# A fused recurrent block on eight cores: the quantisation steps of a period in another order, the absolute value queued one step later

## The chip, the cores and the metric

The kernel runs on the 8 cores of one Trainium2 chip. Each core works on its own 4096 of the 32768 rows; the weights go to all. The metric is the device time in microseconds of the slowest core.

## The reference

Cut to what is computed:

```python
xn = layernorm(x)
# attention half: s
q, k, v = split(rmsnorm(xn) @ qkv_w.T)
q, k = exp(-0.5 * q * q), exp(-0.5 * k * k)
attn = q @ (k.T @ v) / (q @ k.sum() + 1e-6)          # 16 heads, over 2048 rows
s1 = xn + gamma * (attn @ proj_w.T + proj_b)
s  = s1 + gamma * (gelu(rmsnorm(s1) @ conv1_w.T + conv1_b) @ conv2_w.T + conv2_b)
# feed-forward half: g, every operand rounded to a 4-bit grid in blocks of 16
scale = max(max(abs(xb)) / 6, 1e-12)
q4(x) = GRID[searchsorted(MID, abs(xb / scale))] * sign(xb) * scale
h = silu(q4(xn) @ q4(w_gate).T) * (q4(xn) @ q4(w_up).T)
g = silu(q4(h) @ q4(w_down).T)
out = x + s * g
```

## The kernel before

A core holds 32 tiles of 128 rows. The work has three stages.

Stage one, up to about 400 us of the profiled span, makes keys, values and queries (`kv_group`, `q_group`, L628 and L659) with TensorE. ScalarE empties each bank: a square (L643, L676) and an exponential (L645, L679), or a copy (L652). For each x tile VectorE makes statistics (L454 to L457), GpSimd the reciprocal root (L461 to L473), ScalarE the normalised tile (L480), and the SyncE queue transposes it (L484) and loads the next x tile.

Stage two, up to about 1026 us, goes over eight groups of four tiles: `conv1` (L962), `conv2` (L979) and, for the group ahead, attention (L863), its normalisation on VectorE (L882 to L889), the projection (L914) and its sum on VectorE (L921). The projection of a group waits for the last L889 of that group's tiles, since both use the same banks.

Stage three is the feed-forward half: gate and up (L1168), the product of both on VectorE (L1186), its quantisation, and down (L1213).

The 4-bit rounding runs as a stream of tasks beside this. A task is one tile of 128 x 1024 or 128 x 768, of a weight or of x, and takes seven VectorE steps in two halves. `stage1`, with its tile called y (buffer xf): the block maximum (L238), the scale (L242), its reciprocal (L245), the division (L247). Then ScalarE makes the absolute value (`coarse`, L256) into gam. `stage2`: a sum that rounds (L266), the remainder (L269), the product with the scale (L272) into ob. `period` (L278) mixes the first half of one task (a) with the second half of the task before (b) by a string of letters, one per step; `mid`, `late_in` and the sending of the finished tile are called at fixed places in it. A buffer xf is free for the next load once L269 is done.

In stages one and two the main program calls `pump(ns)` (L401) between its own groups. It hands out steps until their costs, which each step yields in ns, use up the credit. So every queue's order is fixed when the program is written, and an instruction waits in its engine's queue behind those that were queued before it. There are 85 tasks in these two stages. In stage three `run` takes whole periods; `late[0]` is true there, and `mid` queues the absolute value. A task made from h has a step ahead of L238 (the product of gate and up), so its first half has five steps; 15 tiles of x are quantised only in this stage, with four.

Of the kernel before, what the change touches and what calls it, by code (L numbers as in the profile page):

```python
# [33 lines left out]
class Sched:  # L34
# [29 lines left out]
    def opt(self, name):  # L64

        return name if name in self.ev else None


def build():
# [15 lines left out]
    with ExitStack() as es:  # L85
# [123 lines left out]
        late = [False]  # L209
# [5 lines left out]
        def xbuf(k):  # L215
            return xf4 if xslot(k) == 3 else xf[xslot(k)]

        def xfree(k):

            had = [j for j in range(max(k - 4, 0), k) if xslot(j) == xslot(k)]  # L220
            return opt("q_nq%d" % had[-1]) if had else None


        def bc(ap, nb):
            return ap.rearrange("p n -> p n ()").broadcast_to([P, nb, 16])

        def blk(ap):
            return ap.rearrange("p (n b) -> p n b", b=16)

        def stage1(k, W, first, src_ev):  # L230

            nb = W // 16
            y = xbuf(k)[:, 0:W]
            am, sc_, rc = (z[k % 2][:, 0:nb] for z in (q_am, q_sc, q_rc))
            if first is not None:
                first()
                yield 1250
            S.add("v", lambda v: v.tensor_reduce(am, blk(y), AX, op.max,  # L238
                                                 apply_absolute_value=True),
                  waits=[src_ev, xfree(k)], ev="q_am%d" % k)  # L240
            yield W * 1.06 + 160
            S.add("v", lambda v: v.tensor_scalar(sc_, am, 1.0 / 6.0, 1e-12, op.mult, op.max),  # L242
                  waits=["q_am%d" % k, opt("q_out%d" % (k - 2))], ev="q_sc%d" % k)
            yield 200
            S.add("v", lambda v: v.reciprocal(rc, sc_), waits=["q_sc%d" % k], ev="q_rc%d" % k)  # L245
            yield 700
            S.add("v", lambda v: v.scalar_tensor_tensor(blk(y), blk(y), TIE, bc(rc, nb),  # L247
                                                        op.mult, op.mult),
                  waits=["q_rc%d" % k], ev="q_y%d" % k)
            if not late[0]:  # L250
                coarse(k, W)
            yield W * 1.06 + 160

        def coarse(k, W):

            S.add("sc", lambda s: s.activation(gam[k % 2][:, 0:W], xbuf(k)[:, 0:W], AF.Abs,  # L256
                                               scale=BIG),
                  waits=["q_y%d" % k, opt("q_out%d" % (k - 2))], ev="q_g%d" % k)

        def stage2(k, W, dst, dst_free, post):  # L260

            nb = W // 16
            y = xbuf(k)[:, 0:W]
            sc_ = q_sc[k % 2][:, 0:nb]
            gm_ = gam[k % 2][:, 0:W]
            S.add("v", lambda v: v.scalar_tensor_tensor(y, gm_, FLOOR, y, op.max, op.add),  # L266
                  waits=["q_g%d" % k, "q_y%d" % k], ev="q_t%d" % k)
            yield W * 1.06 + 160
            S.add("v", lambda v: v.scalar_tensor_tensor(gm_, gm_, FLOOR, y, op.max, op.subtract),  # L269
                  waits=["q_t%d" % k], ev="q_nq%d" % k)  # L270
            yield W * 1.06 + 160
            S.add("v", lambda v: v.scalar_tensor_tensor(blk(dst), blk(gm_), -1.0, bc(sc_, nb),  # L272
                                                        op.mult, op.mult),
                  waits=["q_nq%d" % k] + list(dst_free), ev="q_out%d" % k)
            post(k)
            yield W * 1.06 + 160

        def period(a, b, mid, late_in):  # L278

            a = list_steps(a)  # L280
            b = list_steps(b)
            for n, who in enumerate("aabababa" if a.n == 5 else "aababab"):
                src = a if who == "a" else b
                if n == 1:
                    send()
                    mid()
                if n == 5:
                    late_in()
                c = src.step()
                if c:  # L290
                    yield c
            for src in (a, b):
                while True:
                    c = src.step()
                    if c is None:
                        break
                    yield c
# [22 lines left out]
        def xn_task(tk):  # L320

            if tk["tile"] is not None:
                k = tk["k"]
                buf = xf[k % 3][:, 0:tk["W"]]
                t = tk["tile"]
                S.add("sc", lambda s: s.activation(buf, buf, AF.Identity,
                                                   scale=rstd_all[:, t:t + 1],
                                                   bias=mrs_all[:, t:t + 1]),
                      waits=["q_ld%d" % k, "mrs%d" % t], ev="q_xn%d" % k)
                tk["ev"] = "q_xn%d" % k  # L330
# [3 lines left out]
        def send():  # L334

            while unsent:
                unsent.pop(0)()

        def stored(tk):
            def store(k):  # L340
                S.add("sy", lambda s: s.dma_start(out=tk["dst"], in_=ob[k % 2][:, 0:tk["W"]]),
                      waits=["q_out%d" % k], inc="OB%d" % (k % 2), ev="q_st%d" % k)
                S.ev[tk["done"]] = S.ev["q_st%d" % k]

            def post(k):
                unsent.append(lambda: store(k))
            return post

        def both(cur, prev, ahead=None):

            a = b = None
            if cur is not None:
                k = cur["k"]
                a = (5 if "first" in cur else 4,
                     stage1(k, cur["W"], cur.get("first"), cur["ev"]))
            if prev is not None:
                k = prev["k"]  # L360
                if "post" in prev:
                    dst, post = prev["dst"], prev["post"]
                    free = [opt(e) for e in prev["free"]]
                else:
                    dst, free = ob[k % 2][:, 0:prev["W"]], [opt("q_st%d" % (k - 2))]
                    post = stored(prev)
                b = (3, stage2(k, prev["W"], dst, free, post))
            def late_in():
                if ahead is not None:
                    xn_task(ahead)  # L370

            def mid():
                if prev is not None and "q_g%d" % prev["k"] not in S.ev:
                    coarse(prev["k"], prev["W"])

            for c in period(a, b, mid, late_in):
                yield c

        def stream():
# [884 lines left out]
        def run(cur):  # L1264

            for _ in both(cur, prev[0]):
                pass
            prev[0] = cur
# [105 lines left out]
```

How the kernel before makes its waits and increments, by code:

```python
                def body(eng):  # L1324
                    for fn, waits, inc, amt in S.ops[key]:
                        for smn, val in waits:
                            eng.wait_ge(sems[smn], val)
                        ins = fn(eng)
                        if inc is not None and ins is not None:
                            ins.then_inc(sems[inc], amt)
                    if key == "sy":
                        for smn, val in sorted(S.cnt.items()):
                            eng.wait_ge(sems[smn], val)
```

## Time and profile before

| what | us |
|---|---|
| median of 3 runs | 1955.89 |
| the three runs | 1953.26, 1955.89, 2096.47 |
| the profiled execution | 1954.67 |
| its span on the slowest core (core 4) | 1953.1 |
| spans of the 8 cores | 1941.7 to 1953.1 |

The span runs from the first to the last instruction; the profiled execution's time is 1.6 us longer. Engines: PE is TensorE, PEld its weight loads, DVE VectorE, ACT ScalarE, POOL GpSimd, SPq the SyncE queue. In a row of the timeline "[5.52 <-DVE xf L247]" says that the engine sat idle for 5.52 us before this instruction and that L247 on VectorE ended it.

### The profile page before, as it was taken

The numbers are of one execution on the slowest core, as the hardware profiler recorded it, in microseconds if no ns is written. First come the engines' busy times: TensorE is split into PE (matmuls) and PEld (weight loads), VectorE is DVE, ScalarE is ACT, GpSimd is POOL, SyncE is SP. The second block draws the span as 40 slices with busy tenths as digits, with TensorE's granted clock in tenths as the row PEclk, the third lists the DMA queues.
The fourth block names the chain that finished last, engine by engine and source line by source line (L and its number), as shares of the span: only waits on it lengthen the run. The fifth ranks groups of instructions, "written<-read, shape, count | busy, mean of one in ns | idle before, by whom it ended". The sixth has DMA issues, their size and how long they took to land.

```text
span 1953.1 us, 27578 instructions; the slowest of 8 cores (1941.7 to 1953.1 us)
## 1 busy us (share of the span) xinstructions
PE 1852.0 (95%) x8982; PEld 876.4 (45%) x9142; DVE 1631.1 (84%) x1907; ACT 784.9 (40%) x991; POOL 396.5 (20%) x356
## 2 busy tenths in 40 slices
PE   6899999688999999999999999999999999999997
PEld 3344444344444444444444444444444444444443
DVE  5789999868878878778707999999999999999986
ACT  4577686555353353464312222222232222323221
POOL 3246457444252252252200000000000000000000
PEclk9999999899999999999999999999999999999999
DMA  9899898766546547557699333433343333333322
GB/s 304 217 250 251 226 252 244 209 185 170 149 112 194 144 105 184 151 127 197 155 179 189 99 80 104 104 109 76 105 106 90 91 106 89 92 105 101 85 78 68
DMA packets 367261, 287.06 MB, mean 147 GB/s; under 512 B 299024, under 2 KB 308240, under 8 KB 366096
## 3 DMA queue, kind: packets, MB, share of 16 engines
q1 hardware_dynamic: 367120, 285.29, 56.3%
q8 instruction: 75, 1.23, 0.3%
q14 instruction: 66, 0.54, 0.1%
HBM read 153.63 MB, written 59.24 MB: 109 GB/s over the span
## 4 chain that ended last, share of the span: by engine, by line
PE 76%; DVE 6%; issue 6%; DMA 6%; POOL 2%; ACT 2%; SPq 1%; DVEq 0%; ACTq 0%; POOLq 0%
PE PS L1168 31%; PE PS L1213 15%; PE PS L979 11%; PE PS L962 9%; PE PS L914 5%; DMA xa<-x 2%; PE PS L703 1%; PE PS L637 1%; PE PS L671 1%; DVE q_am L238 1%; DVE ob L272 1%; DVE xf L247 1%; DMA wst<-c1T 1%; DMA wqg_h<-ob 1%; PE PS L863 1%
## 5 line engine op out<-in xcount | busy, mean ns | idle before, releaser
L256 ACT ACTIVATE gam<-xf 128x1024 bf16<-128x1024 f32 (+1 forms) x196 | 198.2, 1011 | 502.1 <-DVE xf L247 493.5
L1168 PE MATMUL PS<-wg,xqT 128*128 128x512 bf16 (+1 forms) x1504 | 318.2, 361 | 3.4 <-DVE so L989 1.7
L1168 PE MATMUL PS<-wu,xqT 128*128 128x512 bf16 (+1 forms) x1510 | 317.5, 361 | 1.4
L266 DVE SCALAR_TENSOR_TENSOR xf<-gam,xf 128x1024 f32<-128x1024 bf16 (+1 forms) x196 | 240.5, 1227 | 38.2 <-ACT gam L256 37.9
L272 DVE SCALAR_TENSOR_TENSOR ob<-gam,q_sc 128x1024 bf16<-128x1024 bf16 (+1 forms) x196 | 240.1, 1225 | 4.4 <-DVE gam L269 2.8
L238 DVE TENSOR_REDUCE q_am<-xf 128x64 f32<-128x1024 f32 (+1 forms) x196 | 227.6, 1161 | 18.6 <-DMA xf<-w_gate 4.0
L247 DVE SCALAR_TENSOR_TENSOR xf<-xf,q_rc 128x1024 f32<-128x1024 f32 (+1 forms) x196 | 238.7, 1218 | 1.9
L269 DVE SCALAR_TENSOR_TENSOR gam<-gam,xf 128x1024 bf16<-128x1024 bf16 (+1 forms) x196 | 234.1, 1194 | 2.1
L962 PE MATMUL PS<-xn2T,c1T_s 128*128 128x512 bf16 x1024 | 231.9, 381 | 0.0
L1213 PE MATMUL PS<-wdA,hqT 128*128 128x512 bf16 x998 | 225.4, 380 | 1.8 <-DMA hqT<-ob 0.5
L979 PE MATMUL PS<-c2T_s,hdd 128*128 128x512 bf16 x1000 | 220.9, 379 | 1.3
L1168 PEld LDWEIGHTS PS<-wg,xqT 128*128 128x128 bf16 x1536 | 150.3, 98 | 159.1 <-issue 2.1
L1168 PEld LDWEIGHTS PS<-wu,xqT 128*128 128x128 bf16 x1536 | 150.3, 98 | 153.9
L1178 ACT ACTIVATE sg<-PS 128x1024 f32<-128x1024 f32 (+1 forms) x96 | 90.9, 948 | 182.3 <-PE PS L1168 182.3
L979 PEld LDWEIGHTS PS<-c2T_s,hdd 128*128 128x128 bf16 x1024 | 100.1, 98 | 120.9
L1213 PEld LDWEIGHTS PS<-wdA,hqT 128*128 128x128 bf16 x1024 | 100.5, 98 | 119.4 <-issue 3.1
L962 PEld LDWEIGHTS PS<-xn2T,c1T_s 128*128 128x128 bf16 x1024 | 99.4, 98 | 115.4 <-issue 2.2
L671 PE MATMUL PS<-xn1T,qT_s 128*128 128x512 bf16 x512 | 123.8, 394 | 20.4 <-ACT sq L676 12.6
L842 POOL TENSOR_TENSOR xx<-xx,gb 128x1024 f32<-128x1024 f32 x32 | 83.1, 2606 | 220.4 <-ACT xx L838 220.4
L914 PE MATMUL PS<-projT_s,atzT 128*128 128x512 bf16 x496 | 114.2, 383 | 11.1 <-DVE atz L889 7.3
L1186 DVE TENSOR_TENSOR xf<-PS,sg 128x1024 f32<-128x1024 f32 (+1 forms) x96 | 108.5, 1130 | 14.8 <-PE PS L1168 13.5
L637 PE MATMUL PS<-kT_s,xn1T 128*128 128x512 bf16 x424 | 105.6, 401 | 12.0 <-ACT xn L480 4.2
(91 smaller groups left out, 1840.8 us busy)
## 6 DMA issues: line engine op xcount, KB each, us to landing
xx<-x SPq DMA_DIRECT2D x32, 512.0 KB, 5.1
xf<-x SPq DMA_DIRECT2D x32, 512.0 KB, 4.4
xr<-x SPq DMA_DIRECT2D x32, 512.0 KB, 4.4
out<-xr SPq DMA_DIRECT2D x31, 512.0 KB, 3.2
xa<-x SPq DMA_DIRECT2D x30, 512.0 KB, 6.2
stg<-qkvT SPq DMA_DIRECT2D x24, 512.0 KB, 13.0
xf<-w_gate SPq DMA_DIRECT2D x22, 512.0 KB, 7.9
xf<-w_up SPq DMA_DIRECT2D x22, 512.0 KB, 6.4
```

Of the source, the lines that this page charges most:

```text
L238: S.add("v", lambda v: v.tensor_reduce(am, blk(y), AX, op.max, apply_absolute_value=True), waits=[src_ev, xfree(k)], ev="q_am%d" % k)
L247: S.add("v", lambda v: v.scalar_tensor_tensor(blk(y), blk(y), TIE, bc(rc, nb), op.mult, op.mult), waits=["q_rc%d" % k], ev="q_y%d" % k)
L256: S.add("sc", lambda s: s.activation(gam[k % 2][:, 0:W], xbuf(k)[:, 0:W], AF.Abs, scale=BIG), waits=["q_y%d" % k, opt("q_out%d" % (k - 2)) ...
L266: S.add("v", lambda v: v.scalar_tensor_tensor(y, gm_, FLOOR, y, op.max, op.add), waits=["q_g%d" % k, "q_y%d" % k], ev="q_t%d" % k)
L269: S.add("v", lambda v: v.scalar_tensor_tensor(gm_, gm_, FLOOR, y, op.max, op.subtract), waits=["q_t%d" % k], ev="q_nq%d" % k)
L272: S.add("v", lambda v: v.scalar_tensor_tensor(blk(dst), blk(gm_), -1.0, bc(sc_, nb), op.mult, op.mult), waits=["q_nq%d" % k] + list(dst_fr ...
L671: S.add("pe", lambda pe, ic=ic: pe.matmul(bk, qT[:, ic, P * qc:P * (qc + 1)], xn1T[:, h:h + 4, ic, :], start=(ic == 0), stop=(ic == 7)), w ...
L914: S.add("pe", lambda pe, ic=ic, hh=hh, bk=bk: pe.matmul(bank(bk), atzT[:, t % 4, ic, :], projT[:, ic, 512 * hh:512 * (hh + 1)], start=(ic ...
L962: S.add("pe", lambda pe, ic=ic: pe.matmul(bk, c1T[:, ic, P * oc:P * (oc + 1)], xn2T[:, :, ic, :], start=(ic == 0), stop=(ic == 7)), waits= ...
L979: S.add("pe", lambda pe, ic=ic: pe.matmul(bank(bks[hh]), hdd[:, ic, P * (t % 4):P * (t % 4 + 1)], c2T[:, ic, 512 * hh:512 * (hh + 1)], sta ...
L1168: S.add("pe", lambda pe, wts=wts, bi=bi, j=j, b0=b0, ic=ic: pe.matmul(bank(b0 + j, GB[bi][1]), xqT[t % 3][:, ic, :], wts[bi][:, ic, :], st ...
L1213: S.add("pe", lambda pe, kc=kc, hh=hh, wt=wt, b0=b0: pe.matmul(bank(b0 + hh), hqT[t % 2][:, kc, :], wt, start=(kc == 0), stop=(kc == 21)), ...
```

## The change

Two edits. The string of a period whose first half has four steps goes from `aababab` to `aaababb`: the reciprocal comes ahead of the older task's rounding sum, the division ahead of its remainder, and the remainder stands right ahead of its product. Periods with five steps keep their order. In the first two stages the absolute value of a task is no longer queued with its division but one step later, after the older task's remainder and ahead of its product.

```diff
@@ stage1
                   waits=["q_rc%d" % k], ev="q_y%d" % k)
-            if not late[0]:
-                coarse(k, W)
             yield W * 1.06 + 160
@@ period
-        def period(a, b, mid, late_in):
+        def period(a, b, mid, late_in, absolute):
...
-            for n, who in enumerate("aabababa" if a.n == 5 else "aababab"):
+            for n, who in enumerate("aabababa" if a.n == 5 else "aaababb"):
                 src = a if who == "a" else b
                 if n == 1:
                     send()
                     mid()
                 if n == 5:
                     late_in()
+                if n == 6:
+                    absolute()
                 c = src.step()
@@ both
-            for c in period(a, b, mid, late_in):
+            def absolute():
+                if cur is not None and not late[0]:
+                    coarse(cur["k"], cur["W"])
+
+            for c in period(a, b, mid, late_in, absolute):
                 yield c
```

The lines of the changed kernel differ: L254 is its absolute value, L264, L267 and L270 its rounding sum, remainder and product; L238, L242, L245 and L247 keep their numbers.

VectorE in stage one, one period and the start of the next, before (xf and gam are the task's buffers, bst and mv_all the statistics of an x tile):

```order
L238 TENSOR_REDUCE q_am1_46<-xf1_84 128x64
L242 TENSOR_SCALAR q_sc1_48<-q_am1_46 128x64
L266 SCALAR_TENSOR_TENSOR xf0_83<-gam0_87,xf0_83 128x1024
L245 RECIPROCAL q_rc1_50<-q_sc1_48 128x64
L454 BN_STATS bst0_60<-xa0_92 128x6
L456 BN_STATS bst0_60<-xa0_92 128x6
L457 BN_AGGR mv_all_51<-bst0_60 128x2
L269 SCALAR_TENSOR_TENSOR gam0_87<-gam0_87,xf0_83 128x1024
L247 SCALAR_TENSOR_TENSOR xf1_84<-xf1_84,q_rc1_50 128x1024
L272 SCALAR_TENSOR_TENSOR ob0_89<-gam0_87,q_sc0_47 128x1024
```

And the same place in the changed kernel:

```order
L238 TENSOR_REDUCE q_am1_46<-xf1_84 128x64
L242 TENSOR_SCALAR q_sc1_48<-q_am1_46 128x64
L245 RECIPROCAL q_rc1_50<-q_sc1_48 128x64
L264 SCALAR_TENSOR_TENSOR xf0_83<-gam0_87,xf0_83 128x1024
L461 BN_STATS bst0_60<-xa0_92 128x6
L463 BN_STATS bst0_60<-xa0_92 128x6
L464 BN_AGGR mv_all_51<-bst0_60 128x2
L247 SCALAR_TENSOR_TENSOR xf1_84<-xf1_84,q_rc1_50 128x1024
L267 SCALAR_TENSOR_TENSOR gam0_87<-gam0_87,xf0_83 128x1024
L270 SCALAR_TENSOR_TENSOR ob0_89<-gam0_87,q_sc0_47 128x1024
```

The reciprocal now follows the scale it reads and the product follows the remainder it reads; the statistics stay in their place.

ScalarE's queue around the absolute value that starts at 241.30 us in the profile of before (sq, pq and xn1 belong to the key and query groups):

```order
L676 ACTIVATE sq_101<-PS 128x512
L679 ACTIVATE pq0_102<-sq_101 128x512
L652 CAST vext1_100<-PS 128x8x64
L256 ACTIVATE gam0_87<-xf0_83 128x1024
L480 ACTIVATE xn1_1_95<-xa1_93,m1_r_57,vr_r_55 128x1024
L652 CAST vext1_100<-PS 128x8x64
L676 ACTIVATE sq_101<-PS 128x512
```

The same place in the changed kernel, where L683, L686, L659 and L487 are these operations:

```order
L683 ACTIVATE sq_101<-PS 128x512
L686 ACTIVATE pq0_102<-sq_101 128x512
L659 CAST vext1_100<-PS 128x8x64
L487 ACTIVATE xn1_1_95<-xa1_93,m1_r_57,vr_r_55 128x1024
L659 CAST vext1_100<-PS 128x8x64
L254 ACTIVATE gam0_87<-xf0_83 128x1024
L683 ACTIVATE sq_101<-PS 128x512
```

The absolute value has moved behind the normalised tile and a copy. Of the 85 absolute values of the first two stages 52 stand behind one to three more instructions of the main program than before, and 33 stand where they stood. The order on TensorE, GpSimd and the SyncE queue is the same in both kernels.

## Rows read from the trace of the kernel before

**Rows 1.** The page, busy time and share of each engine.

```profile
PE 1852.0 (95%) x8982; PEld 876.4 (45%) x9142; DVE 1631.1 (84%) x1907; ACT 784.9 (40%) x991; POOL 396.5 (20%) x356
```

**Rows 2.** Windows: length, busy of PE, PEld, DVE, ACT, POOL, PE clock, DMA, GB/s.

```profile
60.00:400.00 340.00, 301.91 (x1458) 138.69 (x1481) 303.20 (x344) 240.44 (x354) 169.28 (x180) 0.95 0.88 236
400.00:1026.00 626.00, 600.76 (x2921) 279.80 (x2961) 453.76 (x578) 268.15 (x344) 210.53 (x130) 0.99 0.62 157
1026.00:1953.00 927.00, 909.75 (x4390) 438.57 (x4480) 844.78 (x940) 249.46 (x256) 0.00 (x0) 1.00 0.39 99
```

**Rows 3.** Waits 60 to 400 us: who waited for whom, total us, times, longest.

```profile
PE PS L671 <- ACT sq L676: 12.6, 3, 8.6
...
ACT gam L256 <- DVE xf L247: 35.4, 18, 5.5
...
DVE bst L454 <- DMA xa<-x: 10.4, 3, 5.5
DVE xf L266 <- ACT gam L256: 9.4, 5, 5.3
```

**Rows 4.** Timeline of DVE (start us, us, engine, line, operation): one period of stage one.

```profile
175.53 0.20 DVE L242 TENSOR_SCALAR q_sc<-q_am 128x64 f32<-128x64 f32 x1
175.64 1.22 DVE L266 SCALAR_TENSOR_TENSOR xf<-gam,xf 128x1024 f32<-128x1024 bf16 x1
176.78 0.55 DVE L245 RECIPROCAL q_rc<-q_sc 128x64 f32<-128x64 f32 x1
177.24 1.16 DVE L269 SCALAR_TENSOR_TENSOR gam<-gam,xf 128x1024 bf16<-128x1024 bf16 x1
178.32 1.21 DVE L247 SCALAR_TENSOR_TENSOR xf<-xf,q_rc 128x1024 f32<-128x1024 f32 x1
```

**Rows 5.** Timeline of DVE in stage three, dependent neighbours.

```profile
1734.07 0.96 DVE L269 SCALAR_TENSOR_TENSOR gam<-gam,xf 128x768 bf16<-128x768 bf16 x1
1735.20 0.96 DVE L272 SCALAR_TENSOR_TENSOR ob<-gam,q_sc 128x768 bf16<-128x768 bf16 x1 [0.17 <-DVE gam L269]
...
1741.26 0.20 DVE L242 TENSOR_SCALAR q_sc<-q_am 128x64 f32<-128x64 f32 x1
1741.56 0.55 DVE L245 RECIPROCAL q_rc<-q_sc 128x64 f32<-128x64 f32 x1
```

**Rows 6.** Timeline of ACT and PE in stage one, absolute values and waits.

```profile
241.30 1.06 ACT L256 ACTIVATE gam<-xf 128x1024 bf16<-128x1024 f32 x1 [5.52 <-DVE xf L247]
242.26 1.23 ACT L480 ACTIVATE xn<-xa,m_r,vr_r 128x1024 bf16<-128x1024 f32 x1
...
267.35 1.89 PE L671 MATMUL PS<-xn1T,qT_s 128*128 128x512 bf16 x8 [2.73 <-ACT sq L676]
...
306.84 5.23 PE L671 MATMUL PS<-xn1T,qT_s 128*128 128x512 bf16 x16 [2.57 <-ACT sq L643]
...
367.16 1.06 ACT L256 ACTIVATE gam<-xf 128x1024 bf16<-128x1024 f32 x1 [4.23 <-DVE xf L247]
...
368.85 3.61 PE L671 MATMUL PS<-xn1T,qT_s 128*128 128x512 bf16 x16 [1.23 <-ACT sq L676]
```

**Rows 7.** Timeline of stage two: DVE and PE at two attention tails.

```profile
546.22 3.37 DVE L247 SCALAR_TENSOR_TENSOR xf<-xf,q_rc 128x1024 f32<-128x1024 f32 x1
...
551.79 3.40 PE L914 MATMUL PS<-projT_s,atzT 128*128 128x512 bf16 x15 [2.17 <-DVE atz L889]
...
844.36 1.23 DVE L889 TENSOR_TENSOR atz<-PS,zz 128x1024 bf16<-128x1024 f32 x1 [0.17 <-DVE zz L886]
...
846.80 3.40 PE L914 MATMUL PS<-projT_s,atzT 128*128 128x512 bf16 x15
```

**Rows 8.** Waits of DVE, 500 to 1000 us.

```profile
DVE xx L921 <- PE PS L914: 76.0, 24, 4.0
...
DVE den L882 <- PE PS L863: 3.2, 7, 0.8
...
DVE xf L266 <- ACT gam L256: 1.5, 2, 1.3
```

## The prediction

> **What bounds the kernel now.** I read the page first: TensorE is busy 95% of the span, VectorE 84%, ScalarE 40% [rows 1]. A share over three unlike stages says little, so the next view is the table of windows, cut where the work changes [rows 2]. Stage one (60 to 400 us) has TensorE busy 301.9 of 340 us, at a granted clock of 0.95, and VectorE 303.2, so neither runs through. Stage two (400 to 1026 us) has TensorE busy 600.8 of 626. Stage three (1026 us to the end) has it busy 909.8 of 927, with VectorE at 844.8. What the change can give or take is thus some 38 us of TensorE idle in stage one, 25 in stage two and 17 in stage three, plus what the lower clock costs.
>
> The waits say who holds whom in stage one [rows 3]. ScalarE sat before the absolute value (L256) 18 times, 35.4 us in all, until the division (L247) on VectorE was done. TensorE waited 12.6 us in three pieces for ScalarE's squares (L676), which empty its banks. The timeline joins the two: at 367.16 the absolute value starts after 4.23 us of waiting, and at 368.85 TensorE starts after waiting 1.23 us for the square behind it. At 241.30 the wait was 5.52 us, and behind it in the same queue stands the normalisation that starts at 242.26 [rows 6]. Its transpose feeds TensorE, and the SyncE queue holds weight loads behind that transpose; TensorE waited 2.73 us at 267.35 [rows 6].
>
> **The change on VectorE: the new neighbours.** All seven VectorE steps of a period stay; their order changes. In the old order only the scale (L242) stood right behind the instruction it needs. In the new one the reciprocal (L245) stands right behind the scale it needs, and the last product (L272) right behind the remainder it needs (L269). What that costs the trace shows. Scale to the independent step behind it takes 0.11 us from start to start (175.53 to 175.64), and independent long ones start 0.08 us before the end of the one ahead (177.24 + 1.16 = 178.40, next start 178.32) [rows 4]. In stage three the dependent pairs already exist: scale to reciprocal takes 1741.56 - 1741.26 = 0.30 us, and remainder to product leaves 1735.20 - 1734.07 - 0.96 = 0.17 us idle [rows 5]. So a new scale-reciprocal pair costs 0.30 - 0.11 = 0.19 us, and a new remainder-product pair 0.17 + 0.08 = 0.25 us.
>
> The order of instructions tells how many pairs arise, since other work falls between some of them. Stage one: 37 and 28, so 37 x 0.19 + 28 x 0.25 = 14.0 us. Stage two: 45 and 30, so 16.1 us. Stage three, where only the 15 tiles quantised late use this order: 15 and 15, so 6.6 us. Together 36.7 us more of VectorE time; the bounds of what reaches the end are 0 and all of it.
>
> The row decides this price, for the pairs are in the trace. The Trainium skill (VectorE: DVE Perf Modes, section "The DRAIN you can't avoid") says that a semaphore between two VectorE instructions costs nothing extra, measured on chained copies. By that rule the new neighbours would add 0 instead of 36.7 us. The 0.17 us idle before L272 against an overlap of 0.08 us speaks against it here.
>
> **How much of it counts.** Stage one: VectorE idles there too, and idle time that another engine sets can swallow the gaps. It waited 10.4 us for x tiles and 9.4 us for absolute values [rows 3]. The x loads follow tiles that depend on VectorE's own statistics, so I let half of that swallow gaps, 5.2 us. Of the 9.4 us, one wait of 5.3 us comes from ScalarE standing behind TensorE and its absolute value does not move; the other 4.1 us shrink, because the path on VectorE from division to the rounding (L266) now has the remainder and the reciprocal more in it (1.16 + 0.55 us [rows 4]); I take 3.2. The other edge of this, that the absolute value is queued later, could bring new waits of up to the same size; with the longer path beside it I take nothing.
>
> Then the relief on ScalarE. Of the 85 absolute values of the first two stages 52 move, behind one to three other instructions, and every division stands one VectorE step (1.16 us) earlier in relation to its period. At 241.30 and 367.16 the absolute value moves behind the normalisation and behind a square and an exponential: these start up to 6.5 and 4.2 us earlier, so the TensorE waits of 2.73 and 1.23 us [rows 6] can go. I take these, 4.0 us; bounds 0 and the whole 12.6 us. Stage one: 14.0 - 5.2 - 3.2 - 4.0 = +1.6 us.
>
> Stage two: no wait of TensorE there is for ScalarE; the rows are for VectorE. In each group of four tiles VectorE ends by waiting for the projection (76.0 us in 24 waits [rows 8]), which swallows all gaps before it. What counts is the run from there to the last normalisation of attention (L889), for which TensorE waits before L914: 2.17 us at 551.79 [rows 7]. That run holds 5 and 3 new pairs in the median group, 1.7 us. Against it stand the waits of VectorE inside the run, 3.2 us in 7 for attention and 1.5 for absolute values [rows 8], over six runs. At 844.36 the step ends at 845.59 and TensorE starts its next work only at 846.80 without a wait [rows 7], so a run without a stall has about 1 us to spare. Two runs with a stall and no cover pay 1.3 and 1.1, the others 0.2 or less, one of them because a rounding step moves behind its last L889: +2.5 us. SyncE's order is unchanged, but its x and weight loads wait for L269, now one step (1.2 us) later; three or four buffers cover that, and I count 0.
>
> Stage three: 6.6 us more on VectorE against 82 us of its idle time: 0. Also the steps with a first product keep their order.
>
> Sum: 1.6 + 2.5 = +4.1 us on the profiled execution's 1954.67 us gives 1958.8; that execution lies 1.2 us under the median of 1955.89, which is within the spread. I forecast 1959 us. There is scatter as well: a division took 3.37 us at 546.22 where another takes 1.21 [rows 4, 7], some 2 us right in a tail; the new order changes which step such a delay hits, with either sign. The likeliest case's own range is 1950 to 1970.
>
> **Rivals.** (A) ScalarE's relief wins. VectorE's gaps vanish in its idle time and the three waits of 12.6 us go: 1954.7 - 12.6 = 1942 us. For it: the 35.4 us of waiting are real, and both large ones let something through that TensorE needs. Against: a wait for VectorE in a stage where VectorE is nearly full comes back at the next thing that waits for it, here the statistics.
> (B) The new neighbours cost nothing. Then only what is relieved is left, 3.2 us of VectorE's waits and 4.0 us of TensorE's: 1954.7 - 3.2 - 4.0 = 1947.5 us. For it: in stage one the pairs are new, and rows 5 are from stage three. Against: the same instructions with the same operands make the pairs there. This is what the Trainium skill's rule (VectorE: DVE Perf Modes, "The DRAIN you can't avoid") would come to.
> (C) Slower: VectorE paces every stage. If it had no idle time that swallows, all 36.7 us would reach the end: 1991.4 us. Each new stall can add a stretch at half clock: 16 matmuls took 5.23 us at 306.84 against 3.61 at 368.85 [rows 6], 1.6 us; six tails with one make 9.7, so 2001 us. It decides once VectorE's idle time in a stage is less than its gaps; stage one has 37 us of idle against 14.0, so only a chain through the statistics could bring it there.
> (D) The change does nothing: the order of instructions shows that it does move them, so this can only come as a cancelling of terms, inside the forecast.
>
> **How the numbers follow.** Forecast 0.52; A 0.25; B 0.13; C 0.10, mostly in partial form (half of the 36.7 us, 1973). About what a measurement of this kernel can tell from no change is 2%, 39 us: faster means under 1917, slower over 1995. Faster by that needs more than all of stage one's TensorE idle: 0.01. Slower needs all of C: 0.02. Within: 0.97. The range takes A in from below and the partial C from above: 1940 to 1976.
>
> **What would show it.** In the changed profile: reciprocals 0.30 us behind scales and 0.17 us of idle before L270 (the old L272) about 58 times before 1026 us; VectorE busy time as before, with its idle time smaller elsewhere; ScalarE's wait at L254 (the old L256) before 400 us down from 35.4 to some 20 us; the TensorE wait for L914's counterpart near 551 us some 1 us longer. I am wrong if stage one ends over 5 us earlier (A or B; B if the idle before L270 is absent), or if it ends over 10 us later (C).

## The result and the profile after

| | before | after |
|---|---|---|
| median, us | 1955.89 | 1973.95 (4 runs, 1973.37 to 1974.52) |
| ratio | 1 | 1.0094, 95% interval 1.0077 to 1.0111 |
| the profiled execution, us | 1954.67 | 1973.93 |
| its span on the slowest core, us | 1953.1 (core 4) | 1972.4 (core 0) |
| spans of the 8 cores, us | 1941.7 to 1953.1 | 1964.1 to 1972.4 |

Some executions of a kernel are disturbed and longer; a ratio leaves them out and a median does not, so where the two disagree below, the ratio is to be read.

The change made the kernel about 18 us slower. It was predicted to cost 4 us, so the direction was right and the size was wrong. The time lies inside the whole range of 1940 to 1976 us, whose upper end stood for rival C, and above the 1950 to 1970 us of the likeliest case. By the page, VectorE's busy time rose by 35.4 us against [rows 1], with the same 1907 instructions:

```profile
PE 1851.2 (94%) x8982; PEld 876.1 (44%) x9142; DVE 1666.5 (84%) x1907; ACT 783.8 (40%) x991; POOL 388.4 (20%) x356
```

The windows of the changed kernel answer to [rows 2] (the third ends later, as the kernel does):

```profile
60.00:400.00 340.00, 295.95 (x1426) 136.72 (x1448) 307.70 (x343) 234.63 (x343) 168.81 (x180) 0.94 0.85 230
400.00:1026.00 626.00, 588.48 (x2877) 273.28 (x2917) 479.09 (x576) 274.85 (x355) 204.28 (x130) 0.99 0.62 154
1026.00:1970.00 944.00, 927.63 (x4472) 446.59 (x4562) 850.43 (x945) 247.41 (x256) 0.00 (x0) 1.00 0.40 100
```

In the first window VectorE is 4.5 us busier and has done one instruction less; TensorE has done 32 matmuls fewer. In the second VectorE is 25.3 us busier for two instructions less. So the extra busy time is not more work. Between the two landmarks that follow, the same 574 steps last 487.3 us before and 507.0 us after when their durations are added up, 19.7 us more; the rest is lost overlap, since a step that waits for its neighbour no longer starts before that one's end.

Two landmarks split the loss: the first L889 (here L896) after stage one, and the first product of gate and up (L1186, here L1193), which opens stage three. From the timeline of VectorE, before:

```profile
405.89 1.35 DVE L889 TENSOR_TENSOR atz<-PS,zz 128x384 bf16<-128x384 f32 x3 [4.10 <-DMA phi_h<-pqx]
...
1033.59 1.23 DVE L1186 TENSOR_TENSOR xf<-PS,sg 128x1024 f32<-128x1024 f32 x1 [7.32 <-PE PS L1168]
```

and after:

```profile
415.56 1.35 DVE L896 TENSOR_TENSOR atz<-PS,zz 128x384 bf16<-128x384 f32 x3 [5.80 <-DMA phi_h<-pqx]
...
1052.84 1.23 DVE L1193 TENSOR_TENSOR xf<-PS,sg 128x1024 f32<-128x1024 f32 x1 [7.32 <-PE PS L1175]
```

On these two cores, the slowest of each profiled execution, stage one ends 9.7 us later and stage two takes 9.6 us more. Cores differ by some us, so from here on a landmark is the median over the eight cores. The first stands at 400.5 us before and 413.0 after (+12.5). Stage two, the median of each core's distance between the landmarks, takes 627.8 us before and 637.5 after (+9.6). Each kernel has one profile. The kernels below whose stage one is that of the kernel before end it at 400.0 to 401.4 us, and those with the whole change in it at 409.8 to 413.0, so its cost there is 9 to 12 us. The two pairs that share their stage two, uncut, differ by 0.7 us or less. The last product of gate and up starts 19.6 us later after (1942.0 against 1922.4 us on the two profiled cores), where the first started 19.3 us later: stage three neither adds nor gives back.

The new neighbours look as predicted. One period of stage one after, VectorE's timeline:

```profile
177.28 1.22 DVE L267 SCALAR_TENSOR_TENSOR gam<-gam,xf 128x1024 bf16<-128x1024 bf16 x1
178.67 1.23 DVE L270 SCALAR_TENSOR_TENSOR ob<-gam,q_sc 128x1024 bf16<-128x1024 bf16 x1 [0.17 <-DVE gam L267]
...
182.45 0.14 DVE L242 TENSOR_SCALAR q_sc<-q_am 128x64 f32<-128x64 f32 x1
182.70 0.55 DVE L245 RECIPROCAL q_rc<-q_sc 128x64 f32<-128x64 f32 x1
183.17 1.16 DVE L264 SCALAR_TENSOR_TENSOR xf<-gam,xf 128x1024 f32<-128x1024 bf16 x1
```

The idle 0.17 us stands before L270 55 times ahead of 1026 us. After a scale of 0.20 us the reciprocal starts 0.28 to 0.30 us behind it, 67 times.

The waits of stage one after (60 to 400 us, who waited for whom, total us, times, longest) answer to [rows 3]:

```profile
ACT xn L487 <- POOL mrs_all L480: 30.3, 13, 7.5
...
ACT gam L254 <- DVE xf L247: 20.2, 17, 3.4
...
PE PS L678 <- DMA xn1T<-xn: 11.9, 1, 11.9
DVE xf L264 <- ACT gam L254: 9.7, 5, 6.9
PE PS L644 <- DMA xn1T<-xn: 9.3, 3, 5.6
...
PE PS L678 <- ACT sq L683: 4.5, 1, 4.5
...
DVE bst L461 <- DMA xa<-x: 2.4, 2, 1.8
```

The relief of ScalarE came: its wait before the absolute value fell from 35.4 us [rows 3] to 20.2. But it now waits 30.3 us for the statistics of an x tile before it can normalise, and TensorE waits 21.2 us (11.9 and 9.3) for the transposed tile behind that. The rows for the same two places before are these:

```profile
ACT xn L480 <- POOL mrs_all L473: 11.1, 5, 4.2
```

```profile
PE PS L637 <- DMA xn1T<-xn: 0.7, 2, 0.5
```

Stage two shows something else. VectorE's timeline around 850 us:

```profile
844.64 3.38 DVE L267 SCALAR_TENSOR_TENSOR gam<-gam,xf 128x1024 bf16<-128x1024 bf16 x1
...
849.77 2.51 DVE L270 SCALAR_TENSOR_TENSOR ob<-gam,q_sc 128x1024 bf16<-128x1024 bf16 x1
852.21 1.21 DVE L238 TENSOR_REDUCE q_am<-xf 128x64 f32<-128x1024 f32 x1
...
855.92 3.22 DVE L264 SCALAR_TENSOR_TENSOR xf<-gam,xf 128x1024 f32<-128x1024 bf16 x1
...
860.90 2.55 DVE L247 SCALAR_TENSOR_TENSOR xf<-xf,q_rc 128x1024 f32<-128x1024 f32 x1
```

and GpSimd's of the same time:

```profile
844.48 2.46 POOL L849 TENSOR_TENSOR xx<-xx,gb 128x1024 f32<-128x1024 f32 x1 [27.57 <-ACT xx L845]
848.86 2.35 POOL L849 TENSOR_TENSOR xx<-xx,gb 128x1024 f32<-128x1024 f32 x1 [1.92 <-ACT xx L845]
855.72 2.35 POOL L849 TENSOR_TENSOR xx<-xx,gb 128x1024 f32<-128x1024 f32 x1 [4.51 <-ACT xx L845]
860.02 2.35 POOL L849 TENSOR_TENSOR xx<-xx,gb 128x1024 f32<-128x1024 f32 x1 [1.96 <-ACT xx L845]
```

Each of the four long steps (all but L238) starts while GpSimd adds, and ends a full step after the addition, within 0.16 us: 844.48 + 2.46 = 846.94, plus 1.16 gives 848.10, against an end at 848.02. That fits a step that stands still until GpSimd is done. I call such a step stretched when it took over 0.25 us more than usual. From 400 to 1030 us there are 23 with 32.7 us of excess before, and 34 with 52.1 us after: 19.4 us more. The profiled core of before has the least of its eight cores; the medians over the cores are 36.0 and 52.3 us, 16.3 us more. Stage one has stretched steps too, 31 us before and 33 us after, beside another long step of GpSimd, a product (L568, here L575), so little of its loss comes from them. In TensorE's waits of stage two (400 to 1026 us) this stands before the attention groups, before:

```profile
PE PS L863 <- DVE atz L889: 8.5, 5, 4.6
```

and after:

```profile
PE PS L870 <- DVE atz L896: 21.4, 12, 6.3
```

### The profile page after: what moved, and what is told of

It reads as the page before. It is cut to its first block, busy times and chain, and to the rows that moved or that the text cites. A ratio compares the mean times of both kernels' runs of the same rounds, so it can differ in the third digit from the quotient of the medians.

```text
span 1972.4 us, 27583 instructions; the slowest of 8 cores (1964.1 to 1972.4 us)
## 1 busy us (share of the span) xinstructions
PE 1851.2 (94%) x8982; PEld 876.1 (44%) x9142; DVE 1666.5 (84%) x1907; ACT 783.8 (40%) x991; POOL 388.4 (20%) x356
## 4 chain that ended last, share of the span: by engine, by line
PE 68%; DVE 13%; issue 10%; DMA 4%; ACT 2%; POOL 2%; SPq 1%; DVEq 0%; ACTq 0%; POOLq 0%
PE PS L1175 31%; PE PS L1220 15%; PE PS L986 7%; PE PS L969 6%; PE PS L921 5%; DVE gam L267 2%; DVE q_am L238 2%; PE PS L710 1%; DVE xf L247 1%; DMA phi_h<-pq 1%; DVE xf L264 1%; DVE atz L896 1%; PE PS L678 1%; DVE so L996 1%; DVE ob L270 1%
## 5 line engine op out<-in xcount | busy, mean ns | idle before, releaser
L254 ACT ACTIVATE gam<-xf 128x1024 bf16<-128x1024 f32 (+1 forms) x196 | 197.8, 1009 | 512.9 <-DVE xf L247 512.9
L264 DVE SCALAR_TENSOR_TENSOR xf<-gam,xf 128x1024 f32<-128x1024 bf16 (+1 forms) x196 | 239.6, 1222 | 31.2 <-ACT gam L254 31.2
L270 DVE SCALAR_TENSOR_TENSOR ob<-gam,q_sc 128x1024 bf16<-128x1024 bf16 (+1 forms) x196 | 240.1, 1225 | 17.3 <-DVE gam L267 14.9
L247 DVE SCALAR_TENSOR_TENSOR xf<-xf,q_rc 128x1024 f32<-128x1024 f32 (+1 forms) x196 | 251.3, 1282 | 1.9
L267 DVE SCALAR_TENSOR_TENSOR gam<-gam,xf 128x1024 bf16<-128x1024 bf16 (+1 forms) x196 | 249.9, 1275 | 2.4 <-DVE q_sc L242 0.4
L238 DVE TENSOR_REDUCE q_am<-xf 128x64 f32<-128x1024 f32 (+1 forms) x196 | 227.6, 1161 | 18.2 <-ACT xf L329 4.1
L678 PE MATMUL PS<-xn1T,qT_s 128*128 128x512 bf16 x512 | 122.7, 392 | 16.8 <-DMA xn1T<-xn 11.9
L973 ACT ACTIVATE hdd<-PS,c1b_fm 128x512 bf16<-128x512 f32 x128 | 86.9, 680 | 99.3 <-PE PS L969 99.1
L921 PE MATMUL PS<-projT_s,atzT 128*128 128x512 bf16 x496 | 112.6, 379 | 12.8 <-DVE atz L896 7.6
```

The lines of the kernel that those rows point to most:

```text
L678: S.add("pe", lambda pe, ic=ic: pe.matmul(bk, qT[:, ic, P * qc:P * (qc + 1)], xn1T[:, h:h + 4, ic, :], start=(ic == 0), stop=(ic == 7)), w ...
L921: S.add("pe", lambda pe, ic=ic, hh=hh, bk=bk: pe.matmul(bank(bk), atzT[:, t % 4, ic, :], projT[:, ic, 512 * hh:512 * (hh + 1)], start=(ic ...
```

## The experiments

All twelve ran beside the kernel before on their chip, whose median was 1952.7 us (new order alone, the first run of the later absolute value, and both whole kernels with GpSimd cut), 1954.9 (other neighbours, no neighbours, small steps, change in stage one only) and 1956.6 (the others). "Stage one" is the first landmark and "stage two" the distance between the two, medians over the cores of one profiled execution. "Stretched" is the excess in stage two on the profiled core, and behind it the median over the eight cores.

| kernel | us | ratio, 95% interval | stage one | stage two | stretched |
|---|---|---|---|---|---|
| before | 1955.9 | 1 | 400.5 | 627.8 | 32.7, 36.0 |
| after | 1974.0 | 1.0094, 1.0077 to 1.0111 | 413.0 | 637.5 | 52.1, 52.3 |
| new order alone | 1970.2 | 1.0084, 1.0066 to 1.0102 | 407.0 | 635.9 | 50.2, 47.2 |
| later absolute value alone | 1950.5 | 0.9971, 0.9956 to 0.9987 | 399.8 | 621.9 | 32.5, 31.9 |
| before, GpSimd cut | 1933.8 | 0.9907, 0.9891 to 0.9924 | 400.0 | 606.8 | 0, 0 |
| after, GpSimd cut | 1943.3 | 0.9958, 0.9943 to 0.9974 | 409.8 | 609.1 | 0, 0 |
| other neighbours, late division | 1976.6 | 1.0121, 1.0091 to 1.0151 | 409.9 | 639.4 | 46.6, 42.4 |
| no neighbours | 1982.9 | 1.0037, 1.0014 to 1.0059 | 405.3 | 623.5 | 29.9, 30.9 |
| small steps added | 1990.1 | 1.0188, 1.0159 to 1.0217 | 415.3 | 648.9 | 59.9, 57.7 |
| change in stage one only | 1965.7 | 1.0061, 1.0034 to 1.0087 | 410.0 | 627.1 | 35.8, 33.6 |
| change from stage two on | 1969.3 | 1.0067, 1.0045 to 1.0090 | 401.4 | 638.1 | 47.5, 47.2 |
| the same, GpSimd cut | 1938.1 | 0.9904, 0.9871 to 0.9938 | 400.1 | 610.2 | 0, 0 |
| absolute value two steps later | 1968.8 | 1.0064, 1.0041 to 1.0087 | 405.1 | 636.6 | 46.8, 47.4 |

**The two edits apart.** The new string with the absolute value where the old kernel queues it (ScalarE's order up to the end of stage two is then that of before in all but 8 of some 700 places):

```diff
+            for n, who in enumerate("aabababa" if a.n == 5 else "aaababb"):
                 if n == 5:
                     late_in()
+                    absolute()
-                if n == 6:
-                    absolute()
```

> The new order of VectorE's steps, with the absolute value at the place in ScalarE's queue where it stood before. Theory V (the new order on VectorE costs the time: two dependent pairs per period, and more collisions with GpSimd in stage two): this alone gives the whole loss, 1970 to 1980 us, and the TensorE waits for the attention's normalisation (L896) come to 20 us or more. Rival Q (the absolute value, queued later, holds up what is behind it): this alone is near the kernel before, 1950 to 1962 us.

It took 1970.17 us: the order alone carries nearly all of the loss. TensorE's waits for L896's counterpart were 20.0 us, as expected. In stage one its waits are these, with the square, at 4.7 us, as low as in the changed kernel though the absolute value has not moved:

```profile
PE PS L677 <- DMA xn1T<-xn: 10.4, 1, 10.4
...
PE PS L677 <- ACT sq L682: 4.7, 2, 4.4
...
PE PS L643 <- DMA xn1T<-xn: 4.1, 2, 2.7
```

The other half, the old string with the absolute value one step behind the division:

```diff
-            for n, who in enumerate("aabababa" if a.n == 5 else "aaababb"):
+            for n, who in enumerate("aabababa" if a.n == 5 else "aababab"):
```

> VectorE's steps in the order of before, the absolute value in ScalarE's queue where the change puts it. Theory V: no loss, a small gain from ScalarE's relief, 1945 to 1956 us, with ScalarE's wait before the absolute value under 30 us up to 400 us. Rival Q: 1962 to 1975 us.

Its two shortest runs took 1946.44 and 1947.24 us beside a before of 1952.69, too few for a ratio. The same kernel, run once more:

> The same kernel as in the first look at the absolute value alone: the old string, the absolute value queued one step behind the division. There its one run of use took 1946.44 us and its trace ended stage one 4 us and stage two 7.5 us ahead of before. If that was more than scatter: a ratio of 0.995 to 0.998, its interval below 1. If scatter: an interval that holds 1.

That gave a ratio of 0.9971 (0.9956 to 0.9987), 1950.49 us: this half of the change is a small gain, and the version is faster than both kernels. In stage one no gain can be told from scatter (399.8 against 400.5 us); it is in stage two, 621.9 against 627.8. ScalarE's waits there (400 to 1026 us) read

```profile
ACT gam L254 <- DVE xf L247: 70.3, 15, 7.7
```

where before had

```profile
ACT gam L256 <- DVE xf L247: 99.2, 22, 7.7
```

That these shorter waits are the gain is not shown: the changed kernel has 64.9 us there and is slower, and TensorE's waits for L889 and its counterpart are the same in both kernels, 15.8 us before and 15.6 here.

In the changed order the same edit brings no gain: new order alone against the whole change stands at 407.0 and 635.9 against 413.0 and 637.5 us. The ratios overlap, so only the stage-one figures say that it costs there, by some 3 to 6 us: the two other profiles with the whole change in stage one stand at 410.0 and 409.8 us.

**One step further.** The call goes behind the loop, so the absolute value is queued after the older task's product:

```diff
                 if c:
                     yield c
+            absolute()
```

> The old string, the absolute value queued two steps behind the division, after the product and ahead of the next task's block maximum. If what helps is that ScalarE's other work gets past a waiting absolute value: as good as one step, 1944 to 1950 us, or a little better. If the later absolute value makes the next rounding sum on VectorE wait (between them stand only the block maximum and the scale, 1.3 us): VectorE's waits for gam grow from 9.4 us to over 20 us before 400 us, and the time is 1955 to 1970 us.

It was slower, ratio 1.0064. VectorE's and ScalarE's waits before 400 us show that both ends lose:

```profile
ACT xn L486 <- POOL mrs_all L479: 32.8, 14, 6.0
...
DVE xf L264 <- ACT gam L254: 24.7, 10, 6.2
```

One step is a gain and two are a loss. In stage one the next rounding sum (L264) is then too close behind: VectorE's wait for the absolute value is 24.7 us where it was 9.4. Stage two is 8.8 us longer, with 20.9 us of that wait against 1.5 and with more stretched steps.

**GpSimd's additions cut.** In the kernel before and in the changed kernel the bias additions of the attention and of the convolution half are cut to 8 of 1024 columns; the other columns' sums lack the bias.

```diff
-            S.add("gp", lambda p: p.tensor_tensor(xb[:], xb[:], gb[:], op.add),
+            S.add("gp", lambda p: p.tensor_tensor(xb[:, 0:8], xb[:, 0:8], gb[:, 0:8], op.add),
...
-            S.add("gp", lambda p: p.tensor_tensor(x2b[:], x2b[:], gc2[:], op.add),
+            S.add("gp", lambda p: p.tensor_tensor(x2b[:, 0:8], x2b[:, 0:8], gc2[:, 0:8], op.add),
```

> The kernel before, with GpSimd's two large additions of stage two (gb and gc2 to the x tiles) cut to 8 of 1024 columns; the rest of those sums is left out. Theory V-collision: VectorE's long steps in stage two (32.7 us over their usual time before) all but go, and 3 to 8 us of the time with them: 1945 to 1952 us. It is the base for the next kernel.

> The changed kernel with the same additions cut to 8 columns. If collisions with GpSimd carry about half of the loss, it stands 8 to 12 us over the kernel before with the same cut. If the dependent pairs alone carry it, the distance stays at 18 us or more. If collisions in stage two carry all of it, the distance is what stage one lost, 5 to 6 us.

The cut was expected to gain the kernel before 3 to 8 us and gained 18. It removes more than the stretching, since GpSimd has some 140 us less to do in stage two, so not all of the 18 us need be stretched steps. The gap between old and new shrank from 18 to 9.5 us, and it sits mostly in stage one (409.8 against 400.0 us). Stage two differs by 2.4 us, 609.1 against 606.8, where it differed by 9.6, though the new neighbours are all there.

**Other neighbours, and none.** The string aaabbab has as many dependent neighbours, but others (the remainder behind its rounding sum), and leaves the division late.

```diff
-            for n, who in enumerate("aabababa" if a.n == 5 else "aababab"):
+            for n, who in enumerate("aabababa" if a.n == 5 else "aaabbab"):
```

> The kernel before with the string aaabbab: the division stays one step ahead of the product as before and the absolute value is queued with it, but the reciprocal stands right behind its scale and the remainder right behind its rounding sum. So it has about as many dependent neighbours as the changed kernel and none of its earlier division. Theory V (the dependent neighbours cost VectorE time, and that time reaches the end): about 0.19 + 0.25 us in each of some 80 periods again, 1960 to 1972 us beside a before of about 1953. Theory W (the loss of the changed order comes from where the division and the remainder stand against GpSimd and the buffers, not from neighbours): 1950 to 1956 us.

The string abababa has none.

```diff
-            for n, who in enumerate("aabababa" if a.n == 5 else "aababab"):
+            for n, who in enumerate("aabababa" if a.n == 5 else "abababa"):
```

> The kernel before with the string abababa: no step of a period stands behind the step that it reads. Against before it loses the dependent neighbour pair of block maximum and scale, against the changed kernel two more pairs. The division becomes the last step, the product stands ahead of it. Theory V: 0.1 to 0.2 us a period less on VectorE than before, so 1945 to 1953 us, unless the absolute value that is now queued last makes the rounding sum wait. Theory W: no forecast from the pairs; the time depends on the steps' places, 1953 to 1975 us, since the division is later still.

With other neighbours the loss is the changed kernel's or a little more (1.0121; somewhat over the range expected), so it does not hang on the earlier division. Without neighbours the ratio is 1.0037, a small loss where the theory allowed a small gain: stage two is 4.3 us shorter, stage one 4.8 us longer, and VectorE waits 21.1 us for absolute values before 400 us where it waited 9.4 [rows 3], the exception that the expectation named. The two stages leave 0.5 us; the ratio stands for 7 us, with an interval from 3 to 12, and its profiled execution was the shortest of its runs. So 2 us or more are without a place.

**Small steps added.** The old order, with two small VectorE steps behind each reciprocal of stages one and two:

```diff
+            if not late[0]:
+                S.add("v", lambda v: v.tensor_scalar(am, sc_, 1.0, None, op.mult),
+                      waits=["q_sc%d" % k], ev="q_pad%d" % k)
+                S.add("v", lambda v: v.tensor_scalar(am, am, 1.0, None, op.mult),
+                      waits=["q_pad%d" % k], ev="q_pae%d" % k)
```

> The kernel before, with two small VectorE steps of 128 x 64 behind each reciprocal in the first two stages (they copy the scale into the block maximum's buffer, which nothing reads any more): about 0.3 to 0.5 us more on VectorE in each of 85 tasks, 26 to 42 us in all, with the order of all other steps as before. Theory V: as much VectorE time as the changed kernel's 30 us of gaps in these stages, so 1962 to 1975 us. If VectorE's idle time swallows such time, as my forecast had it: 1953 to 1958 us.

One undisturbed period in its timeline:

```profile
178.61 0.55 DVE L245 RECIPROCAL q_rc<-q_sc 128x64 f32<-128x64 f32 x1
179.08 0.13 DVE L247 TENSOR_SCALAR q_am<-q_sc 128x64 f32<-128x64 f32 x1
179.31 0.19 DVE L249 TENSOR_SCALAR q_am<-q_am 128x64 f32<-128x64 f32 x1
179.43 1.22 DVE L274 SCALAR_TENSOR_TENSOR gam<-gam,xf 128x1024 bf16<-128x1024 bf16 x1
```

From the reciprocal to the next long step it takes 179.43 - 178.61 = 0.82 us; in the kernel before it is 0.46 (176.78 to 177.24 [rows 4]). So 0.36 us times 85 tasks is 31 us, as much as the 30.1 us of new gaps in these stages, with nothing reordered. The time went up by 1.88%, some 37 us, more than the 9 to 22 us expected. VectorE's idle time before 1026 us does not swallow such time: stage one is 14.9 us longer, with 13.7 us of added steps and some 5 us more of stretched ones; stage two is 21.1 us longer, with 17 us added and 22 to 27 us more of stretched ones (59.9 us on the profiled core, 57.7 in the median). How the 21.1 us divide between the two this run can't tell. Thirteen of the 36 stretched steps of stage two are the small steps themselves, and stage one has such a case too, which took 2.11 us instead of 0.13:

```profile
170.32 2.11 DVE L247 TENSOR_SCALAR q_am<-q_sc 128x64 f32<-128x64 f32 x1
```

**One stage at a time.** The change in full for the first 38 tasks only, and for the others only. The absolute value stays with the division where the old string holds.

```diff
-            for n, who in enumerate("aabababa" if a.n == 5 else "aaababb"):
+            for n, who in enumerate("aabababa" if a.n == 5 else "aaababb" if new else "aababab"):
...
-                if n == 6:
+                if n == 6 and new:
                     absolute()
...
-            for c in period(a, b, mid, late_in, absolute):
+            for c in period(a, b, mid, late_in, absolute,
+                            cur is not None and cur["k"] < 38):
```

> The change in full for the first 38 tasks (stage one), and the old string and the old place of the absolute value for all later ones. By the traces of before and after the changed kernel is 6 to 10 us behind at the first attention group and 17 to 20 us behind at the end of stage two. Theory of a chain in each stage: 1959 to 1963 us beside a before of about 1953, so that the rest, 8 to 12 us, belongs to stage two. My forecast's split had +1.6 us for stage one: 1954 to 1956. If a late stage one is swallowed by stage two: 1951 to 1955.

> The old string and the old place of the absolute value for the first 38 tasks, the change in full for all later ones: the complement of the run with the change in stage one alone, which was 0.61% over before (0.34 to 0.87%), some 12 us. If the two stages' losses add up, this one is the rest of the changed kernel's 0.94%: 0.3 to 0.6%, so 6 to 11 us over a before of about 1954. My forecast's step for this stage was +2.5 us. If the loss of stage two arises only where stage one has run late: within 3 us of before.

> The change from the 39th task on only, and GpSimd's bias additions cut to 8 of 1024 columns (the bias is left out of the other columns' sums), to be set beside the kernel before with the same cut, 1933.75 us. Theory X (in stage two the new order costs through VectorE steps that are stretched while GpSimd adds; the gaps alone are swallowed there): 1932 to 1937 us. Theory Y (the 16 us of gaps reach the end by themselves): 1940 to 1946 us.

The stages are separate. The first run lost 9.5 us in stage one and nothing in stage two; the second lost 0.9 us in stage one, which is scatter, and 10.3 us in stage two. Their ratios, 0.61% and 0.67%, are both somewhat over what was expected and add up to more than the 0.94% of the whole change, which their intervals allow. The third, with GpSimd cut, stands beside the kernel before with the same cut: 610.2 against 606.8 us in stage two, and ratios of 0.9904 and 0.9907, too coarse to show 3 us. Its 1938.1 us lies between the ranges of both theories. No core of the kernel before with the cut took over 608.7 us in stage two, and no core of this one under 609.2. So the gaps of stage two alone cost some 2 to 3 us (2.4 and 3.4 in the two pairs), a small part of their 16 us; with GpSimd's additions the same change costs 9.6 to 10.3 us. TensorE's waits for L889's counterpart before the attention groups tell the same: 4.9 us with the cut before, 6.1 and 6.2 with the cut and the change, against 8.5 and 21.4 without the cut. The windows of the two cut kernels (400 to 1026 us), the kernel before first,

```profile
400.00:1026.00 626.00, 616.51 (x3053) 287.30 (x3053) 432.64 (x587) 272.30 (x346) 70.87 (x130) 1.00 0.66 163
```

and the change from stage two on,

```profile
400.00:1026.00 626.00, 613.93 (x3036) 285.70 (x3036) 435.47 (x584) 271.16 (x346) 69.28 (x130) 0.99 0.64 161
```

have VectorE's busy time within 3 us of each other, where the uncut kernels lie 25.3 us apart. Added up between the landmarks, their steps last 454.3 and 454.7 us.

## Why the prediction was wrong, point by point

**The price of a neighbour: right.** 0.19 and 0.25 us came out of the trace, and the new gaps look as forecast (0.17 us of idle 55 times against 58 forecast). Rival B falls with it, and so does, in this kernel, the rule that it rested on (the Trainium skill, VectorE: DVE Perf Modes, "The DRAIN you can't avoid"): the step that waits for its neighbour's semaphore starts 0.17 us after it, where an independent one starts 0.08 us before its end. In the line view of stage one L245 had 0.1 us of idle before it and now has 3.9, and L270 has 4.1 us from L267:

```profile
L270 DVE SCALAR_TENSOR_TENSOR ob<-gam,q_sc 128x1024 bf16<-128x1024 bf16 x36 | 47.0, 1306 | 6.1 <-DVE gam L267 4.1 <-DMA wqg_h<-ob 1.8
...
L245 DVE RECIPROCAL q_rc<-q_sc 128x64 f32<-128x64 f32 x38 | 21.0, 553 | 3.9
```

**Stage one: the sum 14.0 - 5.2 - 3.2 - 4.0 = +1.6 us; measured +12.5 (whole change) and +9.5 (change there alone).** From VectorE's timeline I take the stretch from 60 us to the first landmark, less all waits for other engines: 345.9 - 35.8 = 310.1 us before and 355.6 - 28.8 = 326.8 us after on the profiled cores, which are 9.7 us apart. So VectorE was taken up 16.7 us longer, not 14.0; some 2 us of that are stretched steps. Its waits for others shrank by 7.0 us, where the two terms for that came to 5.2 + 3.2 = 8.4. They were near by luck: the wait for x tiles shrank by 8.0 us (10.4 to 2.4), and the wait for absolute values, which was to lose 3.2 us, grew from 9.4 to 9.7. What failed is the step "I take these, 4.0 us" for ScalarE's relief. It is a saving on TensorE, and it was subtracted from a sum of time on VectorE, in a stage where VectorE's chain (statistics, root, normalised tile, transpose) feeds TensorE. The saving did not come: the later absolute value alone ends stage one at 399.8 against 400.5 us, and on top of the new order it costs 3 to 6 us there. TensorE's 12.6 us for the square (L676) did shrink, to 4.5 for its counterpart, but it is 4.7 in the new order alone as well, where the absolute value has not moved. In its place TensorE waits for the transposed tile, 21.2 us in the changed kernel and 14.5 with the new order alone. ScalarE's wait for the statistics had grown there already, from 11.1 to 25.7 us. The prediction had named this way of losing ("comes back at the next thing that waits for it, here the statistics") as what speaks against rival A, and had kept the 4.0 us all the same. Without that term the sum would have been +5.6; the new order alone ends stage one 6.5 us later.

**Stage two: +2.5 us; measured +9.6.** As a price of the gaps alone the forecast was right in size: with GpSimd's additions cut the new order costs 2.4 and 3.4 us there. The step that failed is the last sentence of the sum, "the new order changes which step such a delay hits, with either sign". The stretched steps were taken as scatter around an unchanged mean, and VectorE's busy time as unchanged. They are not scatter: with the same 64 additions of 128 x 1024 to hit, the excess rose from 32.7 to 52.1 us, and TensorE's waits at the attention groups from 8.5 to 21.4 us. With the additions cut both rises are all but gone, and with them some 7 of the 9.6 us. That cut also relieves GpSimd and leaves more slack, so how much of the 7 us is the stretching by itself is not shown. The wait before L914 near 551 us, where I expected 1 us more than the 2.17 of [rows 7], was 2.10 at its counterpart, while the attention groups ahead of it now wait 1.65 and 0.91 (and one reading of the sum was off by a little: TensorE does wait for ScalarE there, 3.0 us for L652 between 400 and 500 us):

```profile
552.12 0.63 PE L870 MATMUL PS<-kvbd,phq 128*128 128x130 bf16 x8 [1.65 <-DVE atz L896]
552.59 3.61 PE L969 MATMUL PS<-xn2T,c1T_s 128*128 128x512 bf16 x16
557.11 0.63 PE L870 MATMUL PS<-kvbd,phq 128*128 128x130 bf16 x8 [0.91 <-DVE atz L896]
...
563.29 3.40 PE L921 MATMUL PS<-projT_s,atzT 128*128 128x512 bf16 x15 [2.10 <-DVE atz L896]
```

**SyncE: "I count 0".** Its wait for the remainder before 400 us went from 3.6 to 27.7 us:

```profile
SPq L1334 <- DVE gam L267: 27.7, 14, 4.9
```

But stage two shows such a lengthening too (35.6 to 64.4 us, and 33.7 to 60.3 with GpSimd cut, where the new order costs only 2.4 us), and VectorE's waits for weight loads did not grow (5.3 us before L238 in stage one, then 3.9). No run isolates it in stage one, so the 0 stands untested there.

**Stage three: 0; measured 0.3 us.** The term held.

**The rivals.** The time is that of the partial form of C (1973 us), and the chain that it named, through the statistics, is the one that grew in stage one (ScalarE's wait for them from 11.1 to 30.3 us). C's reckoning, half of 36.7 us, is right only by its sum: stage one paid most of its 14.0 us, stage two 2 to 3 of its 16.1 and some 7 more that need GpSimd's additions, stage three nothing. That it came near the measured time is luck. A (the relief wins) did not come. In the old order the later absolute value does gain, but 6 us instead of 12.6 and in stage two, where A had nothing.

## What to carry to other kernels

When two engines feed each other, terms of both don't go into one sum: find which chain the stage ends with, and count relief on the other engine as nothing until that chain has room. Ahead of trusting "either sign" for delays that are seen now and then, count them over the whole trace, sum their excess, and look at who ran beside them; 33 us of stretched steps in stage two were in sight in the trace of before, and cutting the additions beside them gave some 18 us (ratio 0.9907), as much as the whole change lost. And split a change of two edits before judging it: one of these two was a gain.

## What the runs showed of the hardware

A VectorE step that meets a 128 x 1024 float32 addition on GpSimd can stand still until it ends; which steps do depends on what they read. Usual steps of 1.16 to 1.22 us took up to 3.38, and small ones of 0.13 us took 2.11. It hits the steps with two tensor operands in SBUF and the small scalings (L242 and those added). I counted, over all cores of before and after and from 400 to 1030 us, the steps that start at least 0.3 us ahead of the end of a long GpSimd step. Of those with two tensors in SBUF 391 of 408 were stretched and of L242 74 of 82, but none of 611 sums that read a PSUM bank (L921 and its counterpart), none of 158 block maxima (L238, which has one tensor operand and took at most 1.22 us) and no reciprocal. With GpSimd's additions cut there was no stretched step in stage two in any of three kernels. The Trainium skill (SBUF — State Buffer, section "SBUF: two separate sides") has this as an exclusive lock on a port pair that VectorE and GpSimd share, taken for VectorE steps with two inputs in SBUF or in a two-port mode; the rows agree, and the block maximum is the case that the section excepts.

What I had not expected is that the number of hits depends on the order. The kernels with about the old gaps in stage two had 30.9 to 36.0 us of excess in the median over the cores (before, later absolute value, no neighbours, change in stage one only), and those with added ones 42.4 to 57.7 (after, new order alone, other neighbours, small steps, change from stage two on), with 64 long additions in each. The absolute value two steps later has 47.4 with no new gap, but VectorE waited 20.9 us for it there, against 1.5 before. That a pause on VectorE is what lets GpSimd's addition in ahead of the next step would fit all of these. So might a mere shift of the steps against the additions: on the profiled cores 13 divisions (L247) start during an addition after, and 5 before. No run isolates either.
